# A bidirectional selective scan: the dead states' product moved from VectorE to GpSimd, and VectorE's scan put ahead of the direct term

## What is computed

```python
xz = x @ Win.T;  u, z = split(xz)
uc = silu(causal_conv4(u, convw) + convb)
x_dbl = uc @ Wx.T                                # dt part, B (32 states), C (32 states)
dt = softplus(x_dbl[:, :16] @ Wdt.T + bdt)
h[n] = exp(dt * A[n]) * h[n] + dt * uc * B[n]    # a recurrence over the tokens, 32 states n
y = sum over n of h[n] * C[n]  +  uc * Dp
out = (y * silu(z)) @ Wout.T
```

## Time and profile before

| | us |
|---|---|
| median of 3 runs (4269.27 to 4273.1) | 4272.15 |
| the profiled execution, its time | 4265.17 |
| its span, first to last instruction | 4263.7 |
| VectorE busy in the stretch 200 to 2300 us | 2061.17 of 2100 |
| TensorE busy in the same stretch | 1994.42 of 2100 |
| ScalarE, GpSimd busy in it | 1596.96, 1092.17 |

### The profile page before, as it was taken

The page is one execution under the profiler, slowest core; times in us unless marked ns, Lnnn a source line. Parts: engine busy times, 40 slices in busy tenths (PEclk is TensorE's granted clock), DMA queues, the critical chain, the costliest instruction groups (busy, mean ns, idle before and its releaser), DMA issues. The chain is left out here.

```text
span 4263.7 us, 69826 instructions
## 1 busy us (share of the span) xinstructions
PE 3975.5 (93%) x19212; PEld 3002.5 (70%) x19213; DVE 3651.0 (86%) x6958; ACT 2806.3 (66%) x4602; POOL 2313.7 (54%) x1949
## 2 busy tenths in 40 slices
PE   6999999999999999999999779999999699999998
PEld 4666666666666666666666557888887488888887
DVE  7999999999999999999999758887888666666665
ACT  5777777777777777777777656665666344454454
POOL 2554545454554545454554546666666555555555
PEclk8988998898989998898989888888889699999999
DMA  2122211222222221122222212222222355555555
GB/s 70 47 46 43 53 43 43 42 53 43 50 46 43 53 43 44 42 53 43 50 46 43 47 45 93 78 78 79 80 77 76 128 93 86 96 102 97 84 95 85
DMA packets 198461, 272.58 MB, mean 64 GB/s; under 512 B 23377, under 2 KB 143058, under 8 KB 198354
## 3 DMA queue, kind: packets, MB, share of 16 engines
q0 software_dynamic: 94432, 130.60, 17.2%
q1 hardware_dynamic: 100480, 138.48, 11.6%
q10 hardware_dynamic: 3442, 2.21, 0.2%
HBM read 121.07 MB, written 150.14 MB: 64 GB/s over the span
## 5 line engine op out<-in xcount | busy, mean ns | idle before, releaser
L615 PE MATMUL pj<-xt,win 128*128 128x512 f32 x3144 | 937.6, 459 | 95.6 <-DVE uc L803 63.0
L615 PEld LDWEIGHTS pj<-xt,win 128*128 128x128 f32 x3144 | 686.9, 222 | 325.6 <-DVE uc L803 89.8
L1992 POOL DMA_INDIRECT out<-e_y,e_to x272 | 473.3, 1740 | 365.4 <-ACT e_y L2098 305.7
L803 DVE SCALAR_TENSOR_TENSOR uc<-pj,convw,uc 128x511 f32<-128x511 f32 (+2 forms) x780 | 516.7, 728 | 5.4 <-ACT uc L408 5.4
L301 POOL TENSOR_TENSOR r<-r,neg_half 128x4 f32<-128x4 f32 x64 | 75.9, 1186 | 760.7 <-ACT r L384 760.7
L326 POOL TENSOR_TENSOR wk<-v,uc 128x512 f32<-128x512 f32 x260 | 333.2, 1281 | 281.3 <-DVE v L851 280.5
L663 PE MATMUL po<-yz,wout 128*128 128x512 f32 x1024 | 456.5, 599 | 4.6 <-ACT fb L491 4.6
L2043 PE MATMUL e_p<-e_w,e_a 128*128 128x256 f32 x3264 | 416.4, 284 | 0.8 <-DVE e_a L2153 0.8
L2043 PEld LDWEIGHTS e_p<-e_w,e_a 128*128 128x128 f32 x3264 | 393.8, 188 | 11.1 <-DVE e_a L2153 2.8
L2031 PE MATMUL e_p<-e_xt,e_w 128*128 128x512 f32 x1632 | 395.1, 397 | 4.1 <-DVE e_xt L2145 2.4
L663 PEld LDWEIGHTS po<-yz,wout 128*128 128x128 f32 x1024 | 189.3, 190 | 267.8 <-issue 267.8
(11 more groups left out here) (244 smaller groups left out, 9105.5 us busy)
## 6 DMA issues: line engine op xcount, KB each, us to landing
e_x<-expert_in SPq DMA_DIRECT2D x138, 260.0 KB, 2.6
bb<-bc SPq DMA_DIRECT2D x65, 512.0 KB, 5.6
h_rows<-fb POOLq DMA_DIRECT2D x64, 512.0 KB, 6.3
h_rows<-h0c SPq DMA_DIRECT2D x32, 512.0 KB, 2.9
a_h<-h_rows SPq DMA_DIRECT2D x128, 128.0 KB
out<-a_bs SPq DMA_DIRECT2D x128, 128.0 KB
bc<-xd SPq DMA_DIRECT2D x65, 128.0 KB, 2.3
e_w1s<-in_moe_w POOLq DMA_DIRECT2D x9, 512.0 KB, 5.5
```

Source lines behind the costliest of these rows:

```text
L615: i = mm(pj[m][:], win[d][wp][:, k, c:c + P], xt[xp][:, k, :], start=(k == 0 and n == 0), stop=(k == KD - 1 and n == 2))
L803: stt(uc[d][:, m, to], pj[m][:, of], convw[d][:, m, tap:tap + 1], uc[d][:, m, to], ALU.mult, ALU.add).then_inc(S["cv"], 1)
L1992: pool.indirect_dma_start(out=out, out_offset=bass.IndirectOffsetOnAxis(ap=to[n][:, j:j + 1].bitcast(U32), axis=0), in_=y[n][:, j, :], in_ ...
```

## The change

Three things change in `mamba_stage`, in every slot.

1. L867 goes. ScalarE copies the row `S` from PSUM to a new SBUF tile `ssum` (`sum_copy`, after the last taps), and GpSimd makes `qq = wk * ssum`, one instruction of 128x512 for each tile (`dead_inputs(t)`, after `ln_scale` and ahead of `add_rows`). `wk` still holds `dt * uc`, so this is `dt * uc * S`.
2. `sums` becomes `tp = qq * dall + tp`, and the direct term is added behind it by a new function `direct`, tile by tile: `tp = uc * Dp + tp`. It takes the place of L871.
3. On VectorE `scan` and `outputs` come straight after `conv` (and `ln_stats`), ahead of `bc_product`; `sums` and `direct` come behind `xt_low`.

Semaphores follow: `sc_ok` counts ScalarE's copies of the sum, `pq_ok` GpSimd's products; ScalarE's L462 waits for `pq_ok`, because GpSimd now reads `wk` for longer; ScalarE's `v_copy` no longer waits for VectorE's product. `q2_ok` is now given by `direct`.

```diff
+        ssum = sb("ssum", [P, SEQ])
...
+            def dead_inputs(t):
+                for m in range(MD):
+                    pool.wait_ge(S["dtu_ok"], MD * t + m + 1)
+                    pool.wait_ge(S["sc_ok"], t + 1)
+                    pool.tensor_tensor(qq[:, m, :], wk[:, m, :], ssum[:], ALU.mult).then_inc(S["pq_ok"], 1)
...
                     if d == 0:
                         ln_scale(s + 1)
+                    dead_inputs(t)
                     if not first:
                         add_rows(t - 2, d, s - 1)
...
                     if not (isinstance(t, int) and t == 0):
-                        act.wait_ge(S["q_ok"], NP * (t - 1) + m // 2 + 1)
                         act.wait_ge(S["dtu_ok"], MD * (t - 1) + m + 1)
...
                         act.wait_ge(S["tp_ok"], MD * (t - 1) + 2 * h + 2)
+                        act.wait_ge(S["pq_ok"], MD * (t - 1) + 2 * h + 2)
                     act.activation(wk[:, mm, :], y[:, mm, :], ACT.Identity, bias=1.0).then_inc(S["w_ok"], 1)
...
+            def sum_copy(t):
+                act.wait_ge(S["s_ps"], t + 1)
+                if not (isinstance(t, int) and t == 0):
+                    act.wait_ge(S["pq_ok"], MD * t)
+                act.activation(ssum[:], pss[:], ACT.Copy).then_inc(S["sc_ok"], 1)
...
                 last_tap_and_bias(t + 1, 1 - d, range(MD))
+                sum_copy(t)
                 if copies:
...
-            def dead_part(t, d):
-                dve.wait_ge(S["s_ps"], t + 1)
-                dve.wait_ge(S["fl_ok"], 3 * t + 2)
-                for h, mm in pairs():
-                    stt(qq[:, mm, :], over_pair(pss[:]), dall[:], v[:, mm, :], ALU.mult, ALU.mult
-                        ).then_inc(S["q_ok"], 1)
-                for m in range(MD):
-                    dve.wait_ge(S["q_ok"], NP * t + m // 2 + 1)
-                    stt(qq[:, m, :], qq[:, m, :], dp[d][:, m:m + 1], uc[d][:, m, :], ALU.add, ALU.mult
-                        ).then_inc(S["q2_ok"], 1)
...
             def sums(t):
+                dve.wait_ge(S["fl_ok"], 3 * t + 2)
                 for h, mm in pairs():
                     dve.wait_ge(S["hc_ok"], t + 1)
-                    dve.wait_ge(S["q2_ok"], MD * t + 2 * h + 2)
-                    tt(tp[:, mm, :], tp[:, mm, :], qq[:, mm, :], ALU.add).then_inc(S["yv_ok"], 1)
+                    dve.wait_ge(S["pq_ok"], MD * t + 2 * h + 2)
+                    stt(tp[:, mm, :], qq[:, mm, :], dall[:], tp[:, mm, :], ALU.mult, ALU.add).then_inc(S["yv_ok"], 1)
+
+            def direct(t, d):
+                for m in range(MD):
+                    dve.wait_ge(S["yv_ok"], NP * t + m // 2 + 1)
+                    stt(tp[:, m, :], uc[d][:, m, :], dp[d][:, m:m + 1], tp[:, m, :], ALU.mult, ALU.add
+                        ).then_inc(S["q2_ok"], 1)
...
                     if d == 0:
                         ln_stats(s + 1)
-                    dead_part(t, d)
                     scan(t, d)
+                    outputs(t, d)
                     bc_product(t + 1, 1 - d)
-                    outputs(t, d)
                     more_states(t, d)
                     if d == 0:
                         xt_low(s + 1)
                     sums(t)
+                    direct(t, d)
                     gate(t, d)
```

More of the change, by code:

```diff
@@ L145, in mamba_stage @@
           u_ps a_ok z_ps z_ok uc_ok xd_ps xd_ok bc_ok bcast xd_st dt_ps v_ok vc_ok y_ok l_ok w_ok g_ok
-          d0_ok dt_ok dtu_ok tp_ok da_ok h_ok hc_ok q_ok q2_ok yv_ok yz_ok xm_ok qd_ps gt_ok ct_ok cnt_ps
+          d0_ok dt_ok dtu_ok tp_ok da_ok h_ok hc_ok sc_ok pq_ok q2_ok yv_ok yz_ok xm_ok qd_ps gt_ok ct_ok cnt_ps
           fl_ok s_ps o_ps fo_ok sq_ok ss_ps rv_ok rr_ok f_ps fin_ok h1_st acc gt2 e_bc e_da e_tp e_h e_hc e_y""".split()
@@ L653, in state_sum @@
                 if not (isinstance(t, int) and t == 0):
-                    pe.wait_ge(S["q_ok"], NP * t)
+                    pe.wait_ge(S["sc_ok"], t)
                 mm(pss[:], smask0[:], bcp[:], start=True, stop=True).then_inc(S["s_ps"], 1)
@@ L670, in row_squares @@
                 if not last:
-                    pe.wait_ge(S["q_ok"], NP * (t + 2))
+                    pe.wait_ge(S["sc_ok"], t + 2)
                 for j in range(TT):
@@ L900, in more_states @@
                             dve.wait_ge(S["e_hc"], at)
-                            dve.wait_ge(S["q2_ok"], MD * (t + 1))
-                            tt(qq[:, m, :], qq[:, m, :], eh, ALU.add).then_inc(S["e_y"], 1)
+                            dve.wait_ge(S["hc_ok"], t + 1)
+                            tt(tp[:, m, :], tp[:, m, :], eh, ALU.add).then_inc(S["e_y"], 1)
                         dve.reg_add(dve_count, dve_count, 1)
@@ L921, in gate @@
                 for h, mm in pairs():
-                    dve.wait_ge(S["yv_ok"], NP * t + h + 1)
+                    dve.wait_ge(S["q2_ok"], MD * t + 2 * h + 2)
                     tt(yz[:, mm, :], tp[:, mm, :], zs[d][:, mm, :], ALU.mult).then_inc(S["yz_ok"], 1)
```

## The result

The changed kernel takes 4516.53 us (median of 4 runs, 4512.13 to 4521.62) against 4271.56 us for the kernel before on the same chip. The ratio is 1.0581, with a 95% interval of 1.056 to 1.0603: 5.8% or 245 us slower. The profiled execution's span is 4515.0 us against 4263.7.

What follows compares the result with a forecast made beforehand. VectorE's work and the chain TensorE, ScalarE, VectorE were taken to end almost together, twice a pair. 32 pairs of 8.9 us (285 us) on 4265 gave 4550, with 7 us to the median 4557 us; range 4345 to 4650.

Steps and rivals of the forecast that it cites:

- the signs that it named: Changed profile: scans of 2 us and more, `ln_scale` about 4 us later, VectorE idle before `xt_low`, TensorE less busy.
- The slot with `d == 1`: One of a pair's two slots in the scan stage, walked from its taps: 39.3 us instead of 37.3.
- the turn: VectorE's scans and GpSimd's products wait for each other in alternation: about 1.15 us taken for each.
- the residual tile: GpSimd's L308 beside VectorE's softplus, in the slot with `d == 1`: counted as 2.3 us more, as before.
- The slot with `d == 0`: The pair's slot with `xt_low`: late `ln_scale` starts `xn` at 20.7 us; slot 44.0 us instead of 37.2.
- the direct term's place: Four direct-term products on VectorE move behind `xt_low`, where work is paid in full: 2.7 us undisturbed.
- The pair that was walked: Two slots of the kernel before, 37.2 and 37.3 us: a pair was to take 83.3 us instead of 74.5.
- Work on VectorE alone: L867 goes, 2.44 us in each slot; work taken off ahead of a wait only makes the wait longer.
- cover for GpSimd's products: GpSimd's eight products a slot (10.6 us) lie beside PSUM-reading taps (7.9 us) and L867 (2.4 us); the change removes L867.
- The scan and the products don't pass each other: Rival, chance 0.17, claimed they do pass: `ln_scale` on time, still 2.7 us a pair slower, 4359 us.
- VectorE's highest share: Rival, faster, chance 0.05: VectorE sheds its product and the stage follows; 2.44 us in 64 slots, floor 4152 us.
- The upper bound: TensorE's lower clock delays `zs`: `xn` at 22.5 us, 40.5 for the other slot; 11.8 us a pair, 4650 us.

## Why the prediction was right, point by point

**The time.** 4557 us were forecast and 4516.53 measured, in the range of 4345 to 4650; the forecast's mechanism is the one that the runs show. The pair of slots was to grow by 8.9 us and grew by 8.1. (83.3 less 74.5 is 8.8, not 8.9; that slip is worth 3 us.) All the signs that it named are in the profile after: scans of 2.2 us, `ln_scale` late by 3.8 us, a wait of 7.07 us ahead of `xt_low`, none for the logarithm in the `d == 1` slots, TensorE less busy.

**The slot with `d == 1`.** 39.3 us forecast, 38.2 measured. The step that was too dear is the turn: 1.15 us were taken for a scan and 1.15 for a product, and the scans start 2.15 us apart (1014.52, 1016.67 and 1018.82 in the trace after), so a turn of both costs 2.15 and not 2.3. `outputs` ends 19.0 us into the slot (19.6 forecast) and the last product at 21.3 (22.2 forecast). L309, the residual tile, now meets L863 and costs 2.07 us, not 2.3.

**The slot with `d == 0`.** 44.0 forecast, 43.6 measured. `ln_scale` ends at 20.2 (20.6 forecast), `xn` starts at 20.2 (20.7), `sums` starts at 28.7 (29.2). The two reasons were taken apart: `ln_scale` in time gives back 2.8 us, and the direct term's place alone costs 3.35 us in the kernel before, against 2.7 in the sum. Of the 0.65 above it, 0.6 is a wait of ScalarE's `xn` for `ln_scale` (the mean over that run's `d == 0` slots), which meets the scans there.

**The pair that was walked.** Its `d == 1` slot of 37.3 us was longer than the mean one (36.53), which the sum didn't know: it set the forecast against 0.8 us a pair too much. By luck that hid half of the 1.5 us by which the two slots above were forecast too long.

**Work on VectorE alone.** That L867 would bring nothing back was argued from the waits. The run without the product shows it, and more: minus 2.1 us of work gave plus 0.5%. The forecast had named L867 as cover for GpSimd's products and so had half of the reason; that the loss of cover would also make `ln_scale` late, it saw only for the change as a whole.

**The rivals.** The scan and the products don't pass each other: the median scan is 2.22 us in the changed kernel. VectorE's highest share was no guide: with VectorE relieved, the stage got longer. Of the Trainium skill's two rules that were weighed, the one on the page "SBUF — State Buffer" (section "Who interferes with whom") is borne out for scans against 128x512 products. The one on the page "Perfetto Trace Analysis" (section "Identifying the Most-Contended Engine") would have led the wrong way for this product: with VectorE busy for 98% of the stage, taking it off was no gain.

**What was allowed for and not seen.** The upper bound let `zs` be late through TensorE's clock. It is late in 13 of 31 `d == 0` slots, mostly by 1.6 us (it ends 18.3 us into the slot, before 16.7) and at most by 2.6. But `ln_scale` is later still (20.2), so this cost nothing in the changed kernel and only took its part of the gain in the run with the early `ln_scale`.

**What stays open.** Some 245 us are made of 53 us for the products, 81 us that an early `ln_scale` gives back and about 95 us for the direct term's place; together 229 (by the ratios, each within its series, about 49, 78 and 93, together 219). The three were measured in different kernels and need not add up, and how the rest divides was not tried. What `scan` and `outputs` ahead of `bc_product` cost by themselves was not run either.

## What to carry to other kernels

Two engines that lock each other out, as VectorE and GpSimd did here on instructions with two SBUF operands, are one resource: before work moves from one to the other, look at what runs beside it. VectorE's instructions with a PSUM operand were cover for GpSimd, and taking one away cost more than it gave. Find the waits of a busy engine before you shorten it: here work ahead of a wait cost nothing as long as the wait lasted, the same work behind it was paid in full, and moving four instructions past one cost 2%. A short instruction in the way of a long chain (`ln_scale`, four times 128x4) deserves to be placed where it can't wait.

## What the runs showed of the hardware that was not expected

- With products of 4 columns in place of 512, GpSimd's four instructions still take 4.62 us together in the `d == 1` slot: three of them last as long as the scan or the `outputs` beside them (1.11, 1.16 and 2.28 us), one falls between two scans (0.19 us). VectorE's `outputs` beside them takes 2.29 us, as when undisturbed. The one that waited paid for the other's length, so a short instruction was delayed for long and delayed little.
- `row_scale`'s instruction on 128x4 (L302), 1.03 us at its shortest, takes up to 3.91 us in the changed kernel, and ScalarE's `finish` waited 1.16 us for it in the `d == 1` slot shown; VectorE did not wait in its turn there.
- The same twelve products took TensorE 3.0 us in 18 of 31 `d == 0` slots of the changed kernel and 4.2 to 5.5 us in the other 13. Both kinds occur behind idle times of 2.1 to 3.2 us; the granted clock was 0.72 in the stretch around a slow one and 1.00 in the kernel before, where none was slow. What lowers the clock stays open.
